# Second batch summed by scans throughout, with an accumulating DMA for the last add: a windowed ratio in float32

## The reference

```
x_n   = groupnorm(x, 32 groups of 6 channels, over height, width and the 6 channels)
s     = box_sum(x_n, width, 5)                      # window 1 over height: nothing
num   = box_sum(s * s, channels, 20)
d     = box_sum(box_sum(x_n * x_n, width, 5), channels, 20)
norm  = number of rows under the window (5, less at the edges of the width)
out   = x + nan_to_num(num / (d * norm), nan=1)
```

## Time and profile before

| | |
|---|---|
| median of three runs | 382.54 us |
| the profiled execution | 381.17 us, its span 379.5 us |
| busy in the span: PE, DVE, ACT, POOL | 355.8, 298.4, 273.1, 249.5 us |
| adds x + ratio on POOL | 63 of 1820 ns |
| centrings on POOL | 64 of 1829 ns |
| stores | 31 of 768 KB, 2 of 384 KB |

### The profile page before, as it was taken

The page is one execution under the profiler, slowest core; times in us unless marked ns, Lnnn a source line. Parts: engine busy times, 40 slices in busy tenths (PEclk is TensorE's granted clock), DMA queues, the critical chain, the costliest instruction groups (busy, mean ns, idle before and its releaser), DMA issues.

```text
span 379.5 us, 7832 instructions
## 1 busy us (share of the span) xinstructions
PE 355.8 (94%) x2960; PEld 349.5 (92%) x2960; DVE 298.4 (79%) x609; ACT 273.1 (72%) x383; POOL 249.5 (66%) x168
## 2 busy tenths in 40 slices
PE   1999979999999999999869999999999999999982
PEld 1999969999999999999869999999999999999981
DVE  2999964766679999999957877777778877777774
ACT  1455559989999999987726777777777777777751
POOL 4000064887888888887158877788777787777631
PEclk9999999999999999999999999999999999999999
DMA  8999300588999973222202222211222222222214
GB/s 243 327 328 329 105 2 0 168 252 263 290 281 282 287 241 106 85 85 83 85 0 85 85 84 85 82 54 53 64 85 85 83 85 85 83 86 83 66 53 134
DMA packets 66486, 50.84 MB, mean 134 GB/s; under 512 B 912, under 2 KB 66448, under 8 KB 66448
## 3 DMA queue, kind: packets, MB, share of 16 engines
q1 hardware_dynamic: 66448, 50.34, 42.8%
HBM read 25.17 MB, written 25.17 MB: 133 GB/s over the span
## 4 chain that ended last, share of the span: by engine, by line
PE 71%; DVE 7%; ACT 5%; issue 2%; POOL 1%; DVEq 0%; POOLq 0%; ACTq 0%
PE N L529 21%; PE U L520 17%; PE D L529 14%; PE S L520 11%; PE S L529 4%; DVE late_triples L668 3%; PE D L572 3%; ACT xs L455 1%; DVE ratio L776 1%; DVE N L779 1%; ACT q L473 1%; ACT xc L422 1%; POOL xc L358 1%; ACT q L479 1%; DVE ratio L785 1%
## 5 line engine op out<-in xcount | busy, mean ns | idle before, releaser
L364 POOL TENSOR_TENSOR xs<-xs,ratio 128x768 f32<-128x768 f32 x63 | 114.6, 1820 | 63.4 <-DVE ratio L785 63.4
L358 POOL TENSOR_TENSOR xc<-xs,mean_c 128x768 f32<-128x768 f32 x64 | 116.9, 1829 | 44.8 <-DVE mean_c L677 44.8
L776 DVE SCALAR_TENSOR_TENSOR ratio<-D,q 128x768 f32<-128x768 f32 x51 | 48.6, 952 | 43.0 <-ACT q L479 43.0
L785 DVE SCALAR_TENSOR_TENSOR ratio<-ratio,N 128x768 f32<-128x768 f32 x64 | 61.1, 954 | 6.4
L779 DVE SCALAR_TENSOR_TENSOR N<-N,q 128x768 f32<-128x768 f32 x64 | 61.5, 960 | 4.9 <-PE N L529 3.1
L473 ACT ACTIVATE q<-D 128x768 f32<-128x768 f32 x51 | 41.4, 811 | 28.1 <-PE D L529 18.4
L479 ACT ACTIVATE q<-q 128x768 f32<-128x768 f32 x64 | 54.1, 846 | 2.0
L520 PE MATMUL S<-b,xc 128*128 128x128 f32 x432 | 54.0, 275 | 0.0
L529 PE MATMUL N<-b_r,xs 128*128 128x138 f32 (+2 forms) x384 | 52.4, 285 | 0.0
L529 PE MATMUL N<-b,xs 128*128 128x138 f32 (+2 forms) x384 | 51.7, 283 | 0.3 <-DVE ratio L785 0.3
L446 ACT ACTIVATE xs<-S 128x768 f32<-128x768 f32 x36 | 29.2, 812 | 31.5 <-PE S L520 31.5
(11 more groups left out here) (89 smaller groups left out, 452.6 us busy)
## 6 DMA issues: line engine op xcount, KB each, us to landing
out<-xs SPq DMA_DIRECT2D x31, 768.0 KB, 3.8
xs<-x SPq DMA_DIRECT2D x8, 1536.0 KB, 14.8
xs<-x SPq DMA_DIRECT2D x16, 768.0 KB, 5.3
out<-xs SPq DMA_DIRECT2D x2, 384.0 KB, 2.6
```

The costliest lines, as they stand in the source:

```text
L358: nc.gpsimd.tensor_tensor(pairs(xc[:, n % XC_RING, :]), pairs(x_flat(n)), mean, ALU.subtract)\
L364: nc.gpsimd.tensor_tensor(x_flat(n), x_flat(n), ratio[:, n % RATIO_RING, :], ALU.add)\
L776: nc.vector.scalar_tensor_tensor(t1, in_bank(d_bank(n)), -TINY, pairs(q[:, n % Q_RING, :]), ALU.add, ALU.mult).then_inc(t1_ready, 1)
L785: nc.vector.scalar_tensor_tensor(t1, t1, 2.0, in_bank(N), ALU.add, ALU.mult).then_inc(ratio_ready, 1)
```

## The change

Six things are changed:

1. `summed(n)` is true for every duo from 35 to 63 (29 duos, 15 before).
2. The scratch lines of the sums are doubled (`SUM_RING`), the second scan writes to SBUF instead of back into PSUM, and the two scans are no longer linked by a wait. The add of the two halves goes from DVE to POOL (`add_sums`).
3. For duos 32 to 61 POOL no longer adds x and ratio: it issues a DMA from ratio into x with `accum_op=add`. The ratio buffer is free when that DMA has landed (`added`), and the store of duos n and n + 1 waits for t1 of duo n + 4 (the last such store for t1(63)), which itself waited for the DMA of n + 1.
4. At the join PE runs `sum_n(29)` ahead of the average of the means, which goes to bank U; DVE spreads the mean behind t1 of duo 29 instead of behind t2; POOL finishes duo 28 and clears the scratch lines before it waits for the mean.
5. Duo 63 takes banks S and U for D and N, so that `sum_d(63)` needs no t1(62).
6. The tail is done in two halves (`finish_last`), each with its own store of 192 KB.

The core of the diff:

```
...
-        mean_ps = [D[:, 1, 6 * GROUPS:7 * GROUPS], beside[1][:, 0:GROUPS]]
+        mean_ps = [D[:, 1, 6 * GROUPS:7 * GROUPS], U[:, 1, PCOLS:PCOLS + GROUPS]]
...
-            return S if n < SWAPPED and n % 2 else D
+            return S if n < SWAPPED and n % 2 or n == LAST else D
+        def n_bank(n):
+            return U if n == LAST else N
...
-            return FIRST_SUMMED <= n < TOTAL and (n - FIRST_SUMMED) % SUMMED_EVERY == 0
+            return FIRST_SUMMED <= n < TOTAL
         def nth_summed(n):
-            return (n - FIRST_SUMMED) // SUMMED_EVERY
+            return n - FIRST_SUMMED
+        def accumulated(n):
+            return DUOS <= n < TOTAL - STEP_DUOS
...
-                sp.wait_ge(out_ready, n + STEP_DUOS)
+                if accumulated(n):
+                    sp.wait_ge(t1_ready, min(n + STEP_DUOS + RATIO_RING, TOTAL))
+                    if n + STEP_DUOS + RATIO_RING > TOTAL:
+                        wait_added(sp, n + STEP_DUOS - 1)
+                else:
+                    sp.wait_ge(out_ready, n + STEP_DUOS)
...
+                if accumulated(n):
+                    pool.dma_start(x_flat(n), ratio[:, n % RATIO_RING, :], accum_op=ALU.add).then_inc(added[(n - DUOS) % RATIO_RING], 16)
+                    return
...
+            def add_sums(n):
+                k = nth_summed(n)
+                pool.wait_ge(scanned, k + 1)
+                if k >= SUM_RING:
+                    pool.wait_ge(d_ready, n - SUM_RING + 1)
+                nc.gpsimd.tensor_tensor(of_20[k % SUM_RING].rearrange("p (r c) -> p r c", r=PAIR), rows_of(heads[k % SUM_RING]),
+                                        rows_of(ends[k % SUM_RING]), ALU.add).then_inc(of_20_ready, 1)
...
+                    finish(n)
+                    clear_sums()
                     for j in range(len(LATE_SETS)):
                         wait_loaded1(pool, j)
                     pool.wait_ge(mean_ready, 2)
...
-                finish(n)
+                if summed(n + BOX_AHEAD):
+                    add_sums(n + BOX_AHEAD)
+                if m != DUOS:
+                    finish(n)
...
+                if k:
+                    act.wait_ge(scanned, k)
...
-                if summed(n - 1):
-                    pe.wait_ge(of_20_ready, nth_summed(n - 1) + 1)
+                if n == MEAN_AT + BOX_AHEAD + 1:
+                    pe.wait_ge(ssq_ready, 2)
...
+                if n == LAST:
+                    pe.wait_ge(s2_ready, n + 1)
+                elif d_prev(n) >= 0:
...
-                if n == MEAN_AT:
-                    average_late_means()
...
+                if n == MEAN_AT:
+                    average_late_means().then_inc(late_mean_in_psum, 1)
...
-                link(nc.vector.tensor_tensor_scan(rising[:, 0:LINE][:, ::-1], restart, squares_ps[:, 0:LINE][:, ::-1], 0.0,
-                                                  ALU.mult, ALU.add))
-                before = squares_ps[:, C_WIN - 1:C_WIN - 1 + REACH]
-                link(nc.vector.tensor_tensor_scan(before, before, restart[:, 0:REACH], 0.0, ALU.add, ALU.mult))
-                if k:
-                    dve.wait_ge(d_ready, n - SUMMED_EVERY + 1)
-                nc.vector.tensor_tensor(of_20.rearrange("p (r c) -> p r c", r=PAIR), rows_of(squares_ps[:, C_WIN - 1:PADDED]),
-                                        rows_of(rising), ALU.add).then_inc(of_20_ready, 1)
+                if k >= SUM_RING:
+                    dve.wait_ge(of_20_ready, k - SUM_RING + 1)
+                end, head = ends[k % SUM_RING], heads[k % SUM_RING]
+                nc.vector.tensor_tensor_scan(end[:, 0:LINE][:, ::-1], restart, squares_ps[:, 0:LINE][:, ::-1], 0.0,
+                                             ALU.mult, ALU.add)
+                nc.vector.tensor_tensor_scan(head[:, 0:REACH], squares_ps[:, C_WIN - 1:C_WIN - 1 + REACH],
+                                             restart[:, 0:REACH], 0.0, ALU.add, ALU.mult).then_inc(scanned, 1)
...
+                if behind_t1:
+                    behind_t1()
...
+                dve.wait_ge(q_ready, LAST + 1)
+                wait_kept(LAST - RATIO_RING)
+                nc.vector.scalar_tensor_tensor(t1, in_bank(d_bank(LAST)), -TINY, q_of, ALU.add, ALU.mult)\
+                  .then_inc(t1_ready, 1)
+                dve.wait_ge(n_ready, LAST + 1)
+                nc.vector.scalar_tensor_tensor(t2, t2, TINY, q_of, ALU.add, ALU.mult).then_inc(t2_ready, 1)
+                dve.wait_ge(t1_ready, LAST + 1)
+                dve.wait_ge(t2_ready, LAST + 1)
+                for i in range(DUO):
+                    link(nc.vector.scalar_tensor_tensor(t2[:, i, :], t1[:, i, :], 2.0, t2[:, i, :], ALU.add, ALU.mult))
+                    nc.vector.tensor_tensor(rows[:, i, :], rows[:, i, :], t2[:, i, :], ALU.add).then_inc(tail_ready, 1)
...
```

More of the change, by code:

```diff
@@ L32 @@
 TOTAL = BATCH * DUOS
+LAST = TOTAL - 1
 SPAN = [(max(128 * j - C_HI, 0), min(128 * (j + 1) + C_LO, PCOLS)) for j in range(CHUNKS)]
@@ L49 @@
 XC2_SLOT, S2_SLOT, LATE_SLOTS = HALF, HALF + 2, 2
-SUM_SLOT = HALF + 4
-FIRST_SUMMED, SUMMED_EVERY = DUOS + 3, 2
+SUM_SLOT, MORE_SLOT = HALF + 4, RAW + HALF
+FIRST_SUMMED = DUOS + 3
+SUM_RING = 2
 PITCH = C + C_LO
@@ L137, in window_ratio_kernel @@
         sums = xs[:, SUM_SLOT * STEP:(SUM_SLOT + 2) * STEP, :].rearrange("p r c -> p (r c)")
-        padded, restart = sums[:, 0:PADDED], sums[:, PADDED:PADDED + LINE]
-        rising, of_20 = sums[:, 1024:1024 + PADDED], sums[:, 1536:1536 + PCOLS]
-        scale_c = sums[:, 2048:2048 + PCOLS]
+        cut = lambda line, *sizes: [line[:, sum(sizes[:i]):sum(sizes[:i + 1])] for i in range(len(sizes))]
+        padded_0, padded_1, restart, end_0, end_1, head_0, head_1 = cut(
+            sums, PADDED, PADDED, LINE, PADDED, PADDED, PADDED, PADDED)
+        more_sums = xs[:, MORE_SLOT * STEP:(MORE_SLOT + 1) * STEP, :].rearrange("p r c -> p (r c)")
+        of_20_0, of_20_1, scale_c = cut(more_sums, PCOLS, PCOLS, PCOLS)
+        padded, ends, heads, of_20 = (padded_0, padded_1), (end_0, end_1), (head_0, head_1), (of_20_0, of_20_1)
         rows_of = lambda line: line[:, 0:PAIR * PITCH].rearrange("p (r c) -> p r c", r=PAIR)[:, :, 0:C]
@@ L169, in window_ratio_kernel @@
         squares_ready = sem("squares_ready")
+        scanned = sem("scanned")
         of_20_ready = sem("of_20_ready")
+        added = [sem(f"added{i}") for i in range(RATIO_RING)]
         xc_ready = sem("xc_ready")
@@ L303, in _ @@
                 store(t)
[L304 to L309, removed]
+            sp.wait_ge(out_ready, DUOS + 1)
+            sp.dma_start(dram_rows(out, LAST - 1), x_rows(LAST - 1)).then_inc(stored[1], 16)
+            for i in range(DUO):
+                first = ROWS - DROWS + i * PAIR
+                sp.wait_ge(tail_ready, i + 1)
+                sp.dma_start(out[BATCH - 1, first:first + PAIR, :, :].rearrange("h w c -> w h c"),
+                             x_rows(LAST)[:, i * PAIR:(i + 1) * PAIR, :]).then_inc(stored[0], 16)
+            sp.wait_ge(stored[0], 16 * (BATCH * STEPS // 2 + DUO))
             sp.wait_ge(stored[1], 16 * (BATCH * STEPS // 2))
@@ L375, in normalise @@
                 pair = xc_of(n)[:, PCOLS:2 * PCOLS].rearrange("p (r c) -> p r c", r=PAIR)
-                nc.gpsimd.tensor_tensor(rows_of(padded[:, C_LO:PADDED]), pair,
+                nc.gpsimd.tensor_tensor(rows_of(padded[k % SUM_RING][:, C_LO:PADDED]), pair,
                                         scale_c.rearrange("p (r c) -> p r c", r=PAIR), ALU.mult)\
                   .then_inc(scaled_ready, 1)
+            def add_sums(n):
[5 more added lines that the diff above has]
+                                        rows_of(ends[k % SUM_RING]), ALU.add).then_inc(of_20_ready, 1)
             def clear_sums():
                 pool.wait_ge(n_ready, RAW_DUOS)
-                nc.gpsimd.memset(padded, 0.0).then_inc(pool_own, 1)
+                nc.gpsimd.memset(sums[:, 0:SUM_RING * PADDED], 0.0).then_inc(pool_own, 1)
                 nc.gpsimd.memset(restart, 1.0).then_inc(pool_own, 1)
@@ L424, in square_line @@
             def square_line(n):
-                act.wait_ge(scaled_ready, nth_summed(n) + 1)
+                k = nth_summed(n)
+                act.wait_ge(scaled_ready, k + 1)
                 act.wait_ge(us_ready, n)
-                nc.scalar.activation(squares_ps, padded, ACT.Square).then_inc(squares_ready, 1)
+                if k:
+                    act.wait_ge(scanned, k)
+                nc.scalar.activation(squares_ps, padded[k % SUM_RING], ACT.Square).then_inc(squares_ready, 1)
             def keep_u(n):
@@ L570, in sum_d @@
                 if summed(n):
-                    pe.wait_ge(of_20_ready, nth_summed(n) + 1)
-                    mm = nc.tensor.matmul(D[:, 1, 0:PCOLS], b5d[:, :], of_20, start=True, stop=True)
+                    k = nth_summed(n)
+                    pe.wait_ge(of_20_ready, k + 1)
```

(31 more changed lines are left out.)

14 lines of the change are left out of this document (9 added, 5 removed).

## The result

The changed kernel takes 366.94 us (median of four runs, 366.77 to 367.20) against 382.55: ratio 0.9593, 95% interval 0.9576 to 0.9609. Forecast: 367.7, and faster. The profiled execution took 367.20 us with a span of 365.3; the one of before 381.17 and 379.5.

| stretch | before | after | difference | forecast |
|---|---|---|---|---|
| start to root(28) | 181.75 | 182.00 | +0.25 | 0 |
| root(28) to root(31), the join | 23.32 | 19.78 | -3.54 | -3.3 |
| root(31) to root(62) | 161.29 | 151.06 | -10.23 | -10.1 |
| root(62) to the end | 13.10 | 12.42 | -0.68 | -1.4 |

A forecast was written before the change was run, and what follows sets the result against it. PE's instruction list was taken to bound batch 1. Savings of 10.5 (duos), 3.3 (join) and 1.4 (tail) less 0.4 give 14.8 us: 366.4 for the profiled execution, plus 1.37 for the median, 367.7; range 366 to 382.

The forecast's parts named there:

- All duos summed: Batch 1 on PE: 14 more duos summed, each 0.75 us shorter (5.57 to 4.82), saving 10.5 us.
- The 0.4 charged for tightness: Batch 1: 0.4 us in all added because DVE's duo of 4.82 us just fits PE's 4.82.
- h below 1.08: POOL in batch 1: h, the time one accumulating DMA holds POOL, costs nothing up to 1.08 us, 27 us per us above.
- Rival C: POOL: the DMA holds it as long as the add it replaces or longer, 387.7 us at h = 1.82; slower; chance 0.17.
- The sign that was named: POOL: idle time before the DMA, waiting for ratio, says h is hidden; none says B or C.
- B: Rival: POOL becomes the bound by a little, h of 1.1 to 1.6, 373.7 us at 1.3, up to 382; chance 0.16.
- A: The forecast itself: POOL and DVE just hide behind PE, 366.3 to 370 us; chance 0.60.
- The landing: Accumulating DMA in batch 1: 11.6 us for issue and landing against 2.6 for a 384 KB store, so hidden.
- The join: Between the batches: U of duo 32 starts at 194.6 instead of 197.9 us, saving 3.3 us.
- The tail: After D(62): span ends 11.7 us behind its end instead of 13.2, gain 1.5, taken as 1.4 us.
- D: Rival: the DMA's data lands late, above 11.6 us, and t1 waits; about 385 us; chance 0.02.
- E: Rival: DVE is the bound, about 370 to 373 us, chance 0.03; in tail times, E is the end of D(62).

The follow-up runs named there:

- e4: Changed kernel with only every second duo summed (35, 37, ..., 63), the rest of the change kept: 377.12 us.
- e2: Changed kernel with two accumulating DMAs of 192 KB per duo in place of one of 384 KB: 387.13 us.
- e1: Changed kernel with POOL adding x and ratio itself for all duos, no accumulating DMA: 384.42 us, 1.0052 of the kernel before.
- e9: Kernel before the change with only the new join added: 378.04 us, 0.9875 of the kernel before.
- e8: Changed kernel with duo 63 in banks D and N again, so D(63) waits for t1(62); half-size tail stores stay: 368.73 us.
- e7: Changed kernel with the halves added on DVE, the second scan writing to PSUM so one input of the add is there: 380.67 us.
- e6: Changed kernel with POOL's old order at the join, clearing behind the wait for the mean and adding duo 28 after centring duo 32: 369.32 us.
- e10: Kernel before the change with extra unused matmuls filling PE's idle time at the join: 381.17 us, beside 381.51 for the kernel before.
- e3: Changed kernel with the add of the halves put back on DVE, both inputs in SBUF, the DMA kept: 408.72 us.
- e5: Changed kernel with SyncE's stores waiting for the accumulating DMAs' landing instead of t1 of duo n + 4: 366.63 us.
- e12: e5 once more, on the same chip as a rerun of the changed kernel: 366.57 us against 367.15.

## Why the prediction was right, point by point

**All duos summed, -10.5.** Right: 10.2 by the table and by the medians of e4, 10.45 between the traces of e4 and the changed kernel. The duo is 4.82 us. The 0.4 charged for tightness was not needed: DVE waits 0.17 us per duo, since the unlinked scans follow each other after 0.90 us and not 1.01.

**POOL, h below 1.08.** Right, with h = 0.90 by the trace and 0.89 by e2. The choice of the side was luck as much as reasoning: the row that it went by, the issue of 0.37, was wrong by more than double, and the forecast would have been false from h = 1.6. Rival C was as near as one instruction: with 1.8 us (e1's add, e2's two DMAs) the time is 384 to 387, forecast 387.7. The form 27 x (h - 1.08) gives 20 us for e1, measured 17.5. The estimate from the Trainium skill (DMA: Bandwidth & Descriptors, Latency and other measured facts), 1 us, was nearer to h than the row, though what the skill states is the time to the first byte and not a hold of the engine. The sign that was named did not work: no idle time on POOL ahead of the DMA was to say B or C, and there is none, yet PE's row is full (50.00 of 50 us). With a list 0.03 us short of PE's the free lag covers it, and only PE's full row tells A from B.

**The landing.** Hidden, as foretold: 4.1 us, issue included, against 11.6. But "does not fill them" undersold it: the engines' busy share rose from 0.25 to 0.73 while their rate went from 80 to 168 GB/s, so a byte of this DMA took some 1.7 times a stored one's share.

**The join, -3.3.** Right in the trace: -3.5 in its stretch, -3.3 up to root(62) by e9. What I did not see is the scatter: the profiled execution of before kept the clock at 1.00 there, and some of its runs were 1 to 4 us longer.

**The tail, -1.4.** Half, -0.7. The bank change is worth 1.4 (e8). The term that was mis-sized is the queue of stores. The held store of duos 60 and 61 went out at E + 5.8 for 5.5, and the 1.5 MB from there took 6.7 us for 6.2, so the end came at E + 12.5 and not 11.7; the last add was nearly in time (E + 8.9 for 8.7). The accumulating DMAs were not beside it: the last of them had moved its data by 357 us, and this store was issued at 358.6.

**The sum.** For the profiled execution 366.4 forecast, 367.2 measured: 0.8 too low. To the median I added 1.37, the distance in the kernel before; in the changed one the median lies 0.26 under the profiled execution. The errors, 0.8 too low and 1.6 too high, cancelled in part, and that the total came within 0.8 us is luck to this extent. The distance was no constant of the measurement; it was probably the clock loss behind the join, which the change removed, but e6, e9 and e10 only make that likely.

Rivals B, D and E did not occur; E's ground was true, as e7 shows: 0.5 us more on DVE costs 13.7 us.

## What to carry to other kernels

Before a step is taken off the bounding engine, add up the list of each other engine for one turn of the loop, start to start: here three engines came out within 0.2 us, and any one of three moves alone (add on POOL, add on DVE from SBUF, two DMAs) would have made the change a loss. An accumulating DMA is a way to take an elementwise add off GpSimd at the price of one issue; read that price from the start of the next instruction and that one's lengthening, not from the DMA's own row. Where runs scatter and the profile is clean, take more profiles and look at the granted clock behind each idle stretch of TensorE; a run's mean clock does not say where it was lost.

## What the runs showed of the hardware that I had not expected

- An accumulating DMA of 128 rows holds POOL for 0.9 us, whether it carries 384 or 192 KB (changed kernel, e2); part of it shows as 0.3 us on the next instruction (0.6 behind two).
- Its landing takes 4.0 to 4.9 us (medians of the runs) where a 384 KB store took 2.6, and it raises the DMA engines' busy share by 0.48 at one per 4.82 us.
- A DVE add with both inputs in SBUF beside POOL's centring (e3): 1750 ns, for 557 with one input in PSUM (e7).
- The clock fell to 0.50 behind an idle time of PE of 2.27 us (e6) and behind some of 1.90 to 1.97 (e3, e5, e8), and stayed at 1.00 behind others of 2.12 to 2.66 at the same places (e9, e10, e12, the kernel before).
